# A chunked scan on TensorE: C and the masked product as weights, eight moving columns per unit

## What is computed

```python
L = jnp.where(mask, jnp.exp(seg), 0.0)            # seg[l, s] = ac[l] - ac[s]
Yd = jnp.einsum('bcln,bcsn,bhcls,bcshp->bclhp', Cc, Bc, L, xc)
states = jnp.einsum('bcln,bhcl,bclhp->bchpn', Bc, decay_states, xc)
_, prev = jax.lax.scan(step, zeros, (states, chunk_decay))   # carry * d + s
Yo = jnp.einsum('bcln,bchpn,bhcl->bclhp', Cc, prev, jnp.exp(ac))
y = Yd + Yo                                        # then + xs * D, times silu(z)
```

## Time and profile before

| | before |
|---|---|
| median of 3 runs | 2029.85 us (2029.0 to 2035.66) |
| profiled execution | 2026.71 us |
| its span | 2024.9 us |
| mean granted TensorE clock | 0.935 of full speed |
| busy: PE, DVE, ACT, POOL | 1731.2, 1043.7, 901.0, 530.4 us |
| the scan's 64 steps start | 982.8 to 1199.8 us |

### The profile page before, as it was taken

One profiled execution on the slowest core, in us unless ns is written; L12 is line 12 of the kernel. 1 busy time (PEld: TensorE's weight loads), 2 busy tenths in 40 slices (PEclk: granted clock), 3 DMA queues, 4 the chain that ended last, 5 costly groups with the idle time before them and its releaser, 6 DMA issues. The chain is left out here.

```text
span 2024.9 us, 51219 instructions
## 1 busy us (share of the span) xinstructions
PE 1731.2 (85%) x20852; PEld 757.1 (37%) x20852; DVE 1043.7 (52%) x1996; ACT 901.0 (44%) x1198; POOL 530.4 (26%) x692
## 2 busy tenths in 40 slices
PE   5877999997999788779688877699999587699997
PEld 2442333333333232234477772233333232233332
DVE  2446575733555556550366654576754286333341
ACT  3113555553444444354444436255555501555553
POOL 0001232320000144420366661122323065022222
PEclk8898999997999799999799998799999798799998
DMA  6001313210000254328443312113131030233423
GB/s 228 11 11 42 85 42 78 48 43 31 11 0 1 59 120 116 84 57 298 152 128 117 113 62 83 43 43 84 42 84 43 9 33 0 63 82 76 100 58 84
DMA packets 62287, 145.08 MB, mean 72 GB/s; under 512 B 35240, under 2 KB 35240, under 8 KB 57984
## 3 DMA queue, kind: packets, MB, share of 16 engines
q1 hardware_dynamic: 62208, 144.12, 26.6%
HBM read 106.07 MB, written 25.44 MB: 65 GB/s over the span
## 5 line engine op out<-in xcount | busy, mean ns | idle before, releaser
L734 ACT ACTIVATE ARENA<-PS,W 128x1024 f32<-128x1024 f32 x448 | 475.0, 1110 | 331.4 <-PE PS L654 331.4
L585 POOL TENSOR_TENSOR ARENA<-ARENA 128x512 f32<-128x512 f32 x224 | 293.3, 1309 | 1173.5 <-DVE ARENA L869 1170.3
L654 PE MATMUL PS<-ARENA,W 64*128 64x512 f32 x1792 | 460.9, 634 | 0.3 <-ACT ARENA L734 0.3
L666 PE MATMUL PS<-ARENA,W 128*64 128x512 f32 x1792 | 433.9, 605 | 12.4 <-DVE ARENA L869 12.4
L869 DVE SCALAR_TENSOR_TENSOR ARENA<-PS,W,ARENA 128x512 f32<-128x512 f32 x256 | 190.6, 750 | 341.2 <-PE PS L666 280.0
L654 PEld LDWEIGHTS PS<-ARENA,W 64*128 64x128 f32 x1792 | 158.9, 191 | 260.5 <-issue 152.3
L666 PEld LDWEIGHTS PS<-ARENA,W 128*64 128x64 f32 x1792 | 109.0, 136 | 302.5 <-issue 207.6
L1246 DVE TENSOR_TENSOR ARENA<-ARENA 128x1024 f32<-128x1024 f32 x64 | 75.6, 1222 | 69.3 <-PE PS L1179 36.1
L1771 PE MATMUL PS<-ARENA 32*32 32x32 f32 x8448 | 103.6, 197 | 4.5 <-issue 4.2
L1216 ACT ACTIVATE ARENA<-PS 128x1024 f32<-128x1024 f32 x64 | 62.0, 1021 | 93.1 <-PE PS L1169 93.1
L1771 PEld LDWEIGHTS PS<-ARENA 32*32 32x32 f32 x8448 | 92.9, 106 | 8.3 <-issue 5.2
(11 more groups left out here) (216 smaller groups left out, 2128.5 us busy)
## 6 DMA issues: line engine op xcount, KB each, us to landing
ARENA<-scratch_g SPq DMA_DIRECT2D x64, 768.0 KB, 9.6
ARENA<-scratch_g SPq DMA_DIRECT2D x64, 256.0 KB, 4.0
W<-w_dram SPq DMA_DIRECT2D x1, 7307.5 KB, 30.0
ARENA<-XN SPq DMA_DIRECT2D x12, 512.0 KB, 3.5
ARENA<-XN SPq DMA_DIRECT2D x16, 256.0 KB, 2.3
scratch_x<-ARENA SPq DMA_DIRECT2D x8, 512.0 KB, 3.7
scratch_b<-ARENA SPq DMA_DIRECT2D x8, 512.0 KB, 3.8
scratch_z<-ARENA SPq DMA_DIRECT2D x8, 512.0 KB, 4.9
```

Of the source, the lines that this page charges most:

```text
L585: nc.gpsimd.tensor_tensor(SUM[:, k, :], SUM[:, k, :], TMP[:, e % 2, :], ALU.add)\
L654: last = mm(PS[:, (b % 2) * R + r, :], w(layer + "_w1", b * 128, (b + 1) * 128, half(r)), XE[half(r), k, :], start=True, stop=True)
L666: last = mm(PS[half(r), 4 + e % 2, :], w(layer + "_w2", b * C, (b + 1) * C), H[:, b % 4, r * T:(r + 1) * T], start=part == 0, stop=part == ...
L734: f(H[:, b % 4, :], PS[:, (b % 2) * R:(b % 2) * R + R, :].rearrange("p a b -> p (a b)"), ACT.Gelu, bias=w(layer + "_b1", b, b + 1)).then_i ...
```

## The change

Past and mix change sides. In `past` C is the stationary operand and SX moves (32 columns still). In `mix` M is stationary and XD moves with the 8 columns of its unit, with no zeros around it and no sum over units. The results then have the place on the partition and channels along the row, so that the growth is a broadcast of the transposed EAC (`EACT`, made once in the projection by one more transpose on VectorE), `load_growth` and the store of EAC go, VectorE adds mix to the product and turns the sum back by a transpose (`back`) after `keep`; x * D moves to ScalarE (`skip`). The add waits for the product on the same engine, and `gate` also waits for `back`.

```diff
-                            elif (q, u) == (2, 1):
-                                load_growth(sp, 0)
-                            sp.wait_ge(m_acc.sem, m_acc.at(14))
+                            sp.wait_ge(m_acc.sem, m_acc.at(15))
-                            sp.dma_start(eac_dram, EAC).then_inc(m_kept.sem, 16)
                     step(v.transpose(DDT, TAIL))
+                    step(v.transpose(EACT, EAC))
...
-            XD = a.take(2, SQ4, UNITS4 * (CHUNK + HD))
+            XD, SUM = a.take(2, P), a.take(2, P)
...
                         if b + 2 < B:
-                            load_growth(sp, b + 2)
                             load_z(sp, b + 2)
...
+                        pool.wait_ge(c_back.sem, c_back.at(t + 1))
                         pool.wait_ge(c_skipped.sem, c_skipped.at(t + 1))
...
+                    def skip(t):
+                        b, k, now = whole(t)
+                        if t % NB == 0:
+                            act.wait_ge(c_in_x[k].sem, c_in_x[k].at((b // 2 + 1) * 16))
+                        if t > 1:
+                            act.wait_ge(c_summed.sem, c_summed.at(t - 1))
+                        f(YD[:, t % 2, :], XBC[k][:, 0, now], ACT.Copy, scale=w("m_skipd")).then_inc(c_skipped.sem, 1)
...
                         if t + 2 < STEPS:
                             expand(t + 2)
+                        if t > 1:
+                            skip(t - 2)
...
                         dve.wait_ge(c_mixed.sem, c_mixed.at(t + 3))
-                        v.tensor_tensor(OUT[:, k, now], PS[:, MIXED + t % 2, PAST], XBC[k][:, 3, now],
-                                        ALU.mult).then_inc(c_past.sem, 1)
                         if t > 1:
-                            dve.wait_ge(c_summed.sem, c_summed.at(t - 1))
-                        v.scalar_tensor_tensor(YD[:, t % 2, :], XBC[k][:, 0, now], w("m_skipd"),
-                                               PS[:, MIXED + t % 2, MIX], ALU.mult, ALU.add).then_inc(c_skipped.sem, 1)
+                            dve.wait_ge(c_back.sem, c_back.at(t - 1))
+                        v.tensor_tensor(pieces(SUM[:, t % 2, :]), pieces(PS[:, MIXED + t % 2, PAST]),
+                                        EACT[:, n * SQ4:(n + 1) * SQ4, b, :].unsqueeze(3)
+                                        .to_broadcast([P, SQ4, UNITS4, HD]), ALU.mult).then_inc(c_past.sem, 1)
+                        dve.wait_ge(c_past.sem, c_past.at(2 * t + 1))
+                        v.tensor_tensor(SUM[:, t % 2, :], SUM[:, t % 2, :], PS[:, MIXED + t % 2, MIX],
+                                        ALU.add).then_inc(c_past.sem, 1)
+
+                    def back(t):
+                        b, k, now = whole(t)
+                        dve.wait_ge(c_past.sem, c_past.at(2 * t + 2))
+                        v.transpose(OUT[:, k, now], SUM[:, t % 2, :]).then_inc(c_back.sem, 1)
...
                         keep(t)
+                        if t > 1:
+                            back(t - 2)
...
-                                last = mm(PS[g, MIXED + k, t], SX[g, k, j, :], CS[g, k, t], start=True, stop=True)
+                                last = mm(PS[g, MIXED + k, t], CS[g, k, t], SX[g, k, j, :], start=True, stop=True)
...
-                                    last = mm(PS[g, MIXED + k, P + j * CHUNK:P + (j + 1) * CHUNK],
-                                              XD[g, k, j, u * CHUNK:(u + 1) * CHUNK],
+                                    at = j * CHUNK + u * HD
+                                    last = mm(PS[g, MIXED + k, P + at:P + at + HD],
                                               M[g, k, u * P + j * CHUNK:u * P + (j + 1) * CHUNK],
-                                              start=u == 0, stop=u == UNITS4 - 1)
+                                              XD[g, k, at:at + HD], start=True, stop=True)
```

More of the change, by code:

```diff
@@ L119, in build @@
         acc_dram = nc.dram_tensor("scratch_acc", (PARTS, P, S), BF16, kind="Internal").ap()
-        eac_dram = nc.dram_tensor("scratch_eac", (P, S), FP32, kind="Internal").ap()
         end_dram = nc.dram_tensor("scratch_end", (P, NCH), FP32, kind="Internal").ap()
@@ L228, in build @@
         c_in_c = [count(f"c_in_c{k}") for k in range(2)]
-        c_in_e = [count(f"c_in_e{k}") for k in range(2)]
         c_in_s = [count(f"c_in_s{k}") for k in range(2)]
@@ L238, in build @@
         c_skipped = count("c_skipped")
+        c_back = count("c_back")
         c_gated = count("c_gated")
@@ L1290, in load_z @@
             sp.dma_start(XBC[b % 2][:, 4, :], scratch[0][b]).then_inc(c_in_z[b % 2].sem, 16)
[L1292 to L1296, removed]
         def load_segments(sp, b, parts=range(PARTS)):
@@ L1313, in load_scan @@
             load_segments(sp, b)
-            load_growth(sp, b)
             load_z(sp, b)
@@ L1327, in mamba_project @@
                 .rearrange("p (k s) -> p k s", k=PARTS)
-            DTT, DDT = ROWS[:, 0:S], ROWS[:, S:2 * S]
+            DTT, DDT, EACT = ROWS[:, 0:S], ROWS[:, S:2 * S], XBC[0][:, 3, :]
             assert a.used <= SCAN_AT + 5 * S
@@ L1346, in _ @@
                             if (q, u) == (1, 0):
-                                sp.wait_ge(m_kept.sem, m_kept.at((PARTS + 2) * 16))
+                                sp.wait_ge(m_kept.sem, m_kept.at((PARTS + 1) * 16))
                                 load_ends(sp, (0, 1))
@@ L1504, in mamba_scan @@
             DDT = ROWS[:, S:2 * S].rearrange("p (j b u) -> p j b u", j=NCH, b=B)
+            EACT = XBC[0][:, 3, :].rearrange("p (j b u) -> p j b u", j=NCH, b=B)
             SEG, GRAM, OWN, MIXED = 0, 2, 4, 6
@@ L1557, in weigh @@
                         pool.wait_ge(c_mixed.sem, c_mixed.at(t + 1))
-                        places = XD[:, t % 2].rearrange("p j (u c) -> p j u c", c=CHUNK + HD)
-                        nc.gpsimd.tensor_tensor(places[:, :, :, 0:HD], pieces(XT[:, n, :]),
+                        nc.gpsimd.tensor_tensor(pieces(XD[:, t % 2, :]), pieces(XT[:, n, :]),
                                                 DTT[:, n * SQ4:(n + 1) * SQ4, b, :].unsqueeze(3)
@@ L1658, in _ @@
                             expand(t + 2)
+                        if t > 1:
+                            skip(t - 2)
+                    for t in range(STEPS - 2, STEPS):
+                        skip(t)
                 @block.vector
@@ L1711, in total @@
                         b, k, now = whole(t)
[L1712 to L1715, removed]
+                        n = t % NB
+                        if n == 0 and b > 1:
+                            dve.wait_ge(c_stored[k].sem, c_stored[k].at(b // 2 * 16))
                         dve.wait_ge(c_mixed.sem, c_mixed.at(t + 3))
-                        v.tensor_tensor(OUT[:, k, now], PS[:, MIXED + t % 2, PAST], XBC[k][:, 3, now],
-                                        ALU.mult).then_inc(c_past.sem, 1)
                         if t > 1:
-                            dve.wait_ge(c_summed.sem, c_summed.at(t - 1))
-                        v.scalar_tensor_tensor(YD[:, t % 2, :], XBC[k][:, 0, now], w("m_skipd"),
-                                               PS[:, MIXED + t % 2, MIX], ALU.mult, ALU.add).then_inc(c_skipped.sem, 1)
+                            dve.wait_ge(c_back.sem, c_back.at(t - 1))
[9 more added lines that the diff above has]
+                        v.transpose(OUT[:, k, now], SUM[:, t % 2, :]).then_inc(c_back.sem, 1)
                     turn(0)
@@ L1733, in _ @@
                         keep(t)
+                        if t > 1:
+                            back(t - 2)
                     for t in range(STEPS - 2, STEPS):
                         total(t)
+                        back(t)
                     fold_gain(dve)
```

## The result

The changed kernel takes 2094.86 us (2092.16 to 2097.53, 4 runs), the one before 2032.44 (2029.0 to 2035.66): the ratio is 1.0307, 95% interval 1.028 to 1.0335. It is slower by 62 us where 40 were forecast. The profiled execution took 2097.5 us, its span is 2095.7, against 2024.9.

What follows compares the result with a forecast made beforehand. TensorE's stream of small matmuls was taken to bound the scan. 41.6 - 1.5 + 1.1 - 0.85 + 0.4 = +40.8 us on 2026.7 gave 2067.5, forecast as 2070 us; own range 2058 to 2085, widened 2036 to 2104.

Steps and rivals of the forecast that it cites:

- D: Scan: TensorE's clock rises for a part, in stretches without transfers, saving about half of the 40 us: 2050 us; chance 0.12.
- Rival E: Mix in the scan: no shorter at 1.2 GHz for eight columns, 31 + 1.5 us more: 2103 us; chance 0.04.
- (2): TensorE's clock in the scan: at 1.2 GHz from start to end, 60 steps taking 242.2 us against 200.6, +41.6 us.
- Rival A: Scan: TensorE's clock stays high as in the kernel before: 2021.8 us, as a median 2025; chance 0.13.
- (1): Mix with eight moving columns: 1.13 us at either clock, gaining 0 at 2.4 GHz and 0.52 us a step at 1.2 GHz.
- Stalls: Mix in the scan, where transfers are issued: 8 us of stalls kept in the 60 steps, bounds 0 and 12.
- (3): Growth loads and the EAC store gone: stalls in mix of six steps fall, -3.4 us at most, inside the 8 kept.
- (4): VectorE in the scan: 3.00 us a step with its wait and transpose, hidden behind 3.88 us steps, cost 0.
- rival C: Scan: the clock stays high and VectorE takes over with steps of 3.2 us, 11 us above the high-clock case: 2036; chance 0.04.
- (5): ScalarE's skip, some 0.34 us, and GpSimd's gate waiting for the transpose cost 0; GpSimd's smaller XD memset gives -0.85 us.
- (6): Projection: one more VectorE transpose of 1.25 us, hidden by over 7 us, cost 0.
- (7): Tail: the last sum and transpose come after the last mix, 0.14 + 0.28: +0.4 us.

Runs made afterwards that it cites:

- experiment 1: The changed kernel with 32 moving columns per mix product in place of 8: 2020.79 us, ratio 0.9956 to the kernel before; run again, 2022.09 us, 0.9942.
- experiment 2: The kernel before with only mix's moving columns cut from 32 to 8 of each chunk, old sides and growth loads kept: 2094.39 us, one execution.
- experiment 3: The changed kernel with 16 or 24 moving columns in mix in place of 8: 2074.68 and 2028.68 us, one execution each.
- Experiment 4: The changed kernel with 16 of the 32 columns of each stationary block of mix loaded, still 8 moving columns: 2074.11 us, one execution.
- experiment 6: The changed kernel with 32 moving columns, entry 1's segment loads moved from scan start to projection: 2033.08 us, against 2022.09 without the move.
- experiment 5: The kernel before with growth loaded for the first two batch entries only: 2026.98 us against 2038.27, ratio 0.9958.

## Why the prediction was right and where it was off

The sign and the mechanism held in one half, the clock; the other half, that mix gets shorter at the low clock, failed. The size was short by 22 us in the medians, by 30 in the profiled executions (70.8 measured, 40.8 forecast). The time lies above the forecast's own range of 2058 to 2085 us. It is inside 2036 to 2104 because that range was stretched to take in rivals D and E.

**(2) The clock** was right as stated: low at the start, 0.50 to the end. Experiments 1 and 2 show that the columns of mix alone decide it here, whichever operand moves. The way there was weaker than its outcome. I compared columns per us with those before two falls (1830) and a rise (2000). With 16 columns the clock rose after a step at 1500 per us, under all of these, and fell after one at much the same (experiment 3). That 8 columns would keep it low to the end did not follow from the three figures, and to that extent it was luck. The Trainium skill's rule ("TensorE: Matmul & The Clock Gate", Part 1), that busy matmuls release the clock, did not help if busy is read as issuing: TensorE was busy for 247.1 of 264.3 us by the records, more than the 177.1 of 200.6 before, at half the clock. Rival A is out.

**(1) Mix is the term that was mis-sized.** "With 8 columns I put mix on that floor at either clock: 1.13 us" failed for the low one. Mix with its turn is 1.86 us instead of 1.39, and steps are 4.08 and 4.60 in place of 3.62 and 4.14: 60 x 0.46 = 28 us. One part is a misreading: the 13.0 ns a pair that I took for 1.2 GHz came from a step whose clock rose in mix (0.59 over the step); at 0.50 throughout it is 13.5 by the same count (1.73 us from the first load to the start of the last matmul, over 128). The greater part is the floor. I had read from gram, whose pair takes nearly twice as long at 1.2 GHz with 64 columns, that 32 columns are what is paid for at 32. Experiment 4 shows that the stationary block, 32 columns wide, is what counts. The runs fit two costs side by side, the load and the stream, of which the longer one counts. As an estimate, half of gram's 23.4 ns for 64 columns (0.75 us for 32 pairs) gives 12 ns for a stream of 32 at 1.2 GHz, beside 13.5 for the load. They are nearly equal, so the rows of before could not tell them apart, and the row with the same loads stood at the other clock. Rival E had this outcome with a chance of 0.04, and its bound, 1.65 us, was in the text as one end. The rule of the Trainium skill ("TensorEngine Tiling (Array Packing)", Instruction Overhead) that a free dimension of 1 costs as much as one of 60 gave its number. The traces agree for 8, 16 and 32 columns at 1.2 GHz and for 16 to 32 at 2.4. The rows of before, on which I called it borne out at the fast clock, hold no product below 32 columns. The reason is another, as a product with half the stationary columns is shorter, and a pair with 64 columns takes 13.1 ns against 8.8 even at 2.4 GHz.

**Stalls**: 8 us were kept, 264.3 - 60 x 4.34 - 1.4 = 2.5 were there. The slower steps hide nearly all of them, which I had put at the lower bound. Together, 28 - 5.5 gives the 22 us by which the 60 steps exceed my 242.2.

**The first three steps** took 17.5 us, where 14.9 was forecast (16.35 less 1.5): no gain in mix, and the three stops of experiment 6 together 1.3 us longer (4.4 against 3.0). **Head**: from GpSimd's first memset to the first segment 4.44 us in place of 5.37, -0.93 for -0.85 forecast; but the scan as a whole began 1.3 us later, and in the profiles of this study it begins anywhere from 979 to 991 us. **The 64th step and the drain** cost 2.5 us more (12.6 from 1265.9 to the end of mix, 10.1 before), forecast 1.5. Behind the scan 2.2 us more, forecast 0. Beyond the forecast that is 22 for the 60 steps, 2.6 for the first three, 2.2 for the start, 1.0 for the end of the scan and 2.2 behind it: the 30.

**(3)** The growth loads' stalls were right in place and a little larger than the 3.4 us given as the most: 4.4 us in their six steps (experiment 5). At the low clock they are hidden anyway: in experiment 2, which has these loads, the 13th step takes 4.08 us, as an undisturbed one does. **(4)** VectorE: the add waits 0.04 us after the product, not 0.14, and the transpose back takes 0.30 us, between my bounds. Its step is about 2.8 us, under 3.02, so at the high clock it is hidden as well, as experiment 1 shows: rival C is out. What **(5)** and **(6)** put at nothing cost nothing to be seen; the tail of **(7)** is not told apart from the drain above.

## What to carry to other kernels

Before columns are cut from small matmuls, ask what a product costs at either clock: the load of its weights, the stream of its moving operand, and a floor below both. Here a pair took 8.8 ns at 2.4 GHz with 16 to 32 columns, and at 1.2 GHz the width of the stationary block ruled, so that cutting the stream gained nothing, but it took away what kept the clock up, and every untouched matmul beside it paid. What makes the floor at 2.4 GHz is not shown: no kernel had less stationary there. A comparison with the same count of products and useless columns is one edit; it gave the swap of sides with 32 columns, about 0.5% faster than the kernel before.

## What was not expected of the hardware

- Moving operands that carry nothing of use pay for themselves: 24 more columns in each of 64 products per step, 74 us less in all.
- With 16 moving columns the clock went up and down in stretches of 14 to 100 us in one scan, though every step has the same matmuls; each fall came behind a step that a stall had stretched.
- At 1.2 GHz a pair of load and matmul takes 13.5 ns with 32 stationary columns and 8, 16 or 32 moving ones, and 9.2 with 16 stationary ones (1.17 us from the first to the last of 128).
- In the first two steps TensorE stops after the same number of loads in all ten profiles, for 0.5 to 3.3 us each, whether or not SP issues transfers then. Each stop ends 1.2 to 1.6 us behind the end of a 16 KB transfer on queue 8, called "instruction".
